# Convolution biases moved out of the loop into PSUM presets, projections split straight from PSUM, and a low-part subtraction moved to GpSimd, in the first stage of an attention and sphere-convolution kernel

## What is computed

```python
x_n = _gn(x)                                            # 4 groups of 2 channels
def _mcl(x, Wm, b):  return einsum('bcgw,cfg->bcfw', x, Wm) + b[None, :, :, None]
def _conv(x, w, b, pad): ...                            # 1x7 over positions, mixes the 8 channels, + b per channel
q = _rope(split_heads(_conv(_mcl(x_n, Wq, bq), q_conv_w, q_conv_b, 3)))
k = _rope(split_heads(_conv(_mcl(x_n, Wk, bk), k_conv_w, k_conv_b, 3)))
v = split_heads(_conv(_mcl(x_n, Wv, bv), v_conv_w, v_conv_b, 3))
```

## Time and profile before

| | |
|---|---|
| Three executions | 1257.97, 1248.56, 1256.05 us; median 1256.05 |
| Profiled execution: time, span | 1258.79 us, 1256.9 us |
| TensorE (matmul) busy in the span | 86% |
| VectorE, ScalarE, GpSimd busy | 74%, 53%, 69% |
| Mean granted TensorE clock | 0.963 of 2.4 GHz |
| `front`: from the start to its last store landed | 0 to about 412.6 us |

### The profile page before, as it was taken

One profiled execution on the slowest core, in us unless ns is written; L12 is line 12 of the kernel. 1 busy time (PEld: TensorE's weight loads), 2 busy tenths in 40 slices (PEclk: granted clock), 3 DMA queues, 4 the chain that ended last, 5 costly groups with the idle time before them and its releaser, 6 DMA issues. The chain is left out here.

```text
span 1256.9 us, 26231 instructions
## 1 busy us (share of the span) xinstructions
PE 1079.0 (86%) x10648; PEld 590.9 (47%) x10648; DVE 933.5 (74%) x1225; ACT 663.2 (53%) x1110; POOL 871.2 (69%) x812
## 2 busy tenths in 40 slices
PE   0299999999894699899998999999988589899998
PEld 0177777777673123333333333333333345355553
DVE  3789999999764798788888888888872584544344
ACT  1555555555442066666666666666666223346345
POOL 0467776777583489899998899988999007937900
PEclk9899999999998589999999999999999799899999
DMA  9725244332644555527171736254000599875661
GB/s 305 238 83 161 76 124 116 104 94 67 139 105 99 115 77 126 111 55 116 49 121 35 122 65 114 57 94 81 31 19 18 184 354 299 265 228 155 190 214 54
DMA packets 137759, 159.02 MB, mean 127 GB/s; under 512 B 17852, under 2 KB 85708, under 8 KB 137640
## 3 DMA queue, kind: packets, MB, share of 16 engines
q1 hardware_dynamic: 113448, 119.37, 39.6%
q10 hardware_dynamic: 15648, 28.81, 6.6%
q0 software_dynamic: 8544, 9.18, 2.8%
HBM read 106.48 MB, written 52.89 MB: 127 GB/s over the span
## 5 line engine op out<-in xcount | busy, mean ns | idle before, releaser
L1108 POOL TENSOR_TENSOR a_pl<-a_prob 128x512 bf16<-128x512 f32 x416 | 443.1, 1094 | 37.0 <-ACT a_prob L1059 36.4
L1012 DVE TENSOR_REDUCE a_negmax<-a_row 128x1 f32<-128x512 f32 x512 | 334.1, 706 | 60.4 <-PE a_row L939 59.2
L1059 ACT ACTIVATE a_prob<-a_col 128x512 f32<-128x512 f32 x512 | 292.1, 596 | 147.0 <-PE a_col L960 140.7
L710 POOL TENSOR_TENSOR f_yl<-f_y,f_yh 128x768 bf16<-128x768 f32 x80 | 132.8, 1679 | 95.8 <-ACT f_yh L657 95.8
L657 ACT ACTIVATE f_yh<-f_y 128x768 bf16<-128x768 f32 x80 | 67.4, 844 | 139.1 <-DVE f_y L548 121.2
L1023 DVE TENSOR_TENSOR a_pl<-a_prob 128x512 bf16<-128x512 f32 x96 | 123.3, 1285 | 19.2 <-ACT a_prob L1059 19.2
L450 PE MATMUL f_acc<-f_wh,f_xh 128*32 128x384 bf16 x1280 | 110.9, 335 | 29.8 <-DVE f_wl L538 26.5
L939 PE MATMUL a_row<-k,q 96*128 96x512 bf16 x256 | 106.6, 423 | 22.7 <-PEq L202 14.9
L960 PE MATMUL a_col<-a_q,a_k 98*128 98x512 bf16 x256 | 97.9, 388 | 23.2 <-ACT a_prob L1059 19.3
L960 PE MATMUL a_col<-q,k 98*128 98x512 bf16 x256 | 99.8, 390 | 16.1 <-ACT a_prob L1059 14.7
L714 POOL TENSOR_TENSOR f_straight<-f_straight,f_turned 128x832 f32<-128x832 f32 x40 | 107.0, 2675 | 9.4 <-DVE f_turned L565 9.4
(11 more groups left out here) (156 smaller groups left out, 2189.2 us busy)
## 6 DMA issues: line engine op xcount, KB each, us to landing
X<-b_x ACTq DMA_DIRECT2D x16, 526.0 KB, 8.3
q<-in_x SPq DMA_DIRECT2D x8, 1024.0 KB, 7.7
a_v<-V SPq DMA_DIRECT2D x16, 512.0 KB, 4.4
Z<-a_z ACTq DMA_DIRECT2D x32, 256.0 KB, 3.5
b_z<-Z SPq DMA_DIRECT2D x16, 512.0 KB, 11.0
b_x<-in_x SPq DMA_DIRECT2D x32, 256.0 KB, 10.1
b_res<-X SPq DMA_DIRECT2D x38, 208.0 KB
out<-b_y ACTq DMA_DIRECT2D x38, 208.0 KB
```

The source lines that it names most:

```text
L710: nc.gpsimd.tensor_tensor(yl[half][n % 2][:], y[half][:], yh[half][n % 2][:], ALU.subtract).then_inc(yl_done, 1)
L1012: nc.vector.reduce_max(negmax[n % PAIR][:, 0, t:t + 1], row[step % ROWS][:], AX.X, negate=True).then_inc(max_done, 1)
L1059: nc.scalar.activation(prob[sets_done % RING][:, t % QUAD, :], col[step % 2][:], ACT.Exp).then_inc(exp_done, 1)
L1108: nc.gpsimd.tensor_tensor(pl[p][:, r, :], prob[p][:, r, :], ph[p][:, r, :], ALU.subtract).then_inc(lo_pool, 1)
```

## The change

All in `front`:

1. **Presets.** Three pseudo windows (`KINDS` = inner, last, first position) are put in front of the loop. Their y is the projection's bias alone (masked by `edge` for the two end kinds), split into high and low (`bias_high` on ScalarE, `bias_low` on VectorE) and sent through `convolution(0..2)`, with `bias_rows`. ScalarE copies the results to SBUF (`tile_qk`, `tile_v`, the latter adding the V bias). TensorE runs these three convolutions before `projection(0, 0)`.
2. **The loop's convolution** has no bias matmul (24 instead of 28 for Q and K) and accumulates onto a preset accumulator: ScalarE writes the kept results into PSUM before each window (`place_v(n)`, `place_qk(n)`), after `keep_v(n - 1)` and after the rope products of window n - 1.
3. **y.** `evacuate`, the mask and `y` are gone. ScalarE's `y_high` rounds straight from `acc`; `y_low` moves from GpSimd to VectorE and subtracts from `acc`. So `acc[half]` is free only after `y_low`.
4. **q_low** moves from VectorE to GpSimd, ahead of `rope_sum` in each window. `keep_v` is one plain copy.
5. **Preparation.** Statistics have four buffers, so their four loads wait for nothing; chunk 0 is loaded before `band`; the first four weight loads are issued when the third statistics load has landed (before: the second); weight tiles 4 to 7 are split in between the pseudo windows. The zero columns at the ends are cleared by GpSimd (`clear_pad`), and edge chunks are normalised only where they hold data.

The core of the diff:

```diff
+        KINDS = (None, 1, 0)
+        def turn(n):
+            return n + len(KINDS)
@@ TensorE
-                    pe.wait_ge(y_ready, summed(n - 1, half))
+                    pe.wait_ge(yl_done, 2 * turn(n - 1) + half + 1)
...
+                if tiled and i:
+                    pe.wait_ge(tiled_qk, i)
+                if not tiled:
+                    pe.wait_ge(preset_qk, i - len(KINDS) + 1)
...
-                        nc.tensor.matmul(out, ones16[:], bias_rows[:, a]..., start=True, stop=False)
+                        if tiled:
+                            nc.tensor.matmul(out, ones16[:], bias_rows[:, a]..., start=kf == 0, stop=False, ...)
...
+            for i in range(len(KINDS)):
+                convolution(i)
             for n in range(TOTAL):
                 projection(n, 0)
                 projection(n, 1)
@@ VectorE
-            for c in range(QUAD + 1, C, 2):
-                w_low(c)
             v.wait_ge(bias_in, 16 * (C + 3))
...
+            for i in range(len(KINDS)):
+                for half in range(HALVES):
+                    bias_low(i, half)
+                if i % 2 == 0:
+                    w_low(QUAD + 1 + i)
-            for n in range(TOTAL + 2):
+            for n in range(TOTAL + 1):
                 for half in range(HALVES):
                     if n < TOTAL:
-                        evacuate(n, half)
-                if 1 <= n <= TOTAL:
+                        y_low(n, half)
+                if n:
                     rope_products(n - 1)
-                if n >= 2:
-                    q_low(n - 2)
@@ ScalarE
-            act.wait_ge(x_in[1], 16)
+            act.wait_ge(x_in[2], 16)
...
-            for c in range(C):
+            for c in range(QUAD):
                 w_high(c)
             act.wait_ge(bias_in, 16 * (C + 3))
+            act.wait_ge(edge_in, 16)
+            for i in range(len(KINDS)):
+                for half in range(HALVES):
+                    bias_high(i, half)
+                w_high(QUAD + i)
+                tile_qk(i)
+                tile_v(i)
+            w_high(C - 1)
...
+                if 1 <= n <= TOTAL:
+                    keep_v(n - 1)
+                if n < TOTAL:
+                    place_v(n)
+                    place_qk(n)
@@ GpSimd
+            for n in range(TOTAL + 2):
+                if n >= 2:
+                    q_low(n - 2)
+                if 1 <= n <= TOTAL:
+                    rope_sum(n - 1)
```

More of the change, by code:

```diff
@@ L472, in convolution @@
+                            nc.tensor.matmul(out, yh[half][s][:, feat], band_l[:, half, a, :], start=False, stop=False, skip_group_check=loose)
+                            last = nc.tensor.matmul(out, yl[half][s][:, feat], band_h[:, half, a, :], start=False, stop=half == 1, skip_group_check=loose)
                 last.then_inc(qk_full, 1)
-                if m:
-                    pe.wait_ge(v_kept, 2 * m)
+                if tiled and i:
+                    pe.wait_ge(tiled_v, 2 * i)
+                if not tiled:
+                    pe.wait_ge(preset_v, i - len(KINDS) + 1)
@@ L538, in w_low, with y_low, bias_low @@
                 nc.vector.tensor_tensor(wl[c][:], w[c % 4], wh[c][:], ALU.subtract).then_inc(w_lo[1], 1)
[L540 to L552, removed]
+            def y_low(n, half):
+                s = turn(n) % 2
+                v.wait_ge(yh_done, 2 * turn(n) + half + 1)
+                nc.vector.tensor_tensor(yl[half][s][:].rearrange("p (a n) -> p a n", a=2), acc[half][:, :, 0:PART],
+                                        yh[half][s][:].rearrange("p (a n) -> p a n", a=2), ALU.subtract).then_inc(yl_done, 1)
+            def bias_low(i, half):
+                e = KINDS[i]
+                v.wait_ge(yh_done, 2 * i + half + 1)
+                if e is None:
+                    nc.vector.tensor_tensor(yl[half][i % 2][:], bias[half][:], yh[half][i % 2][:], ALU.subtract).then_inc(yl_done, 1)
+                else:
+                    nc.vector.scalar_tensor_tensor(yl[half][i % 2][:], bias[half][:], edge[:, e:e + 1], yh[half][i % 2][:],
+                                                   ALU.mult, ALU.subtract).then_inc(yl_done, 1)
             def rope_products(m):
@@ new lines, in y_high, with bias_high @@
+                act.wait_ge(v_full, turn(n) - 1)
+                nc.scalar.activation(yh[half][turn(n) % 2][:].rearrange("p (a n) -> p a n", a=2), acc[half][:, :, 0:PART], ACT.Copy).then_inc(yh_done, 1)
+            def bias_high(i, half):
+                e = KINDS[i]
+                if i >= 2:
+                    act.wait_ge(v_full, i - 1)
+                if e is None:
+                    nc.scalar.activation(yh[half][i % 2][:], bias[half][:], ACT.Copy).then_inc(yh_done, 1)
+                else:
+                    nc.scalar.activation(yh[half][i % 2][:], bias[half][:], ACT.Identity, scale=edge[:, e:e + 1]).then_inc(yh_done, 1)
@@ new lines, in tile_qk, with tile_v @@
+            def tile_qk(i):
+                e = KINDS[i]
+                act.wait_ge(qk_full, i + 1)
+                if e is None:
+                    nc.scalar.activation(inner_qk[:], acc_qk[:, :, 0:2 * OC].rearrange("p a (m w) -> p a m w", w=OW)[:, :, :, PAD], ACT.Copy).then_inc(tiled_qk, 1)
+                else:
+                    nc.scalar.activation(edge_qk[e][:], acc_qk[:, :, 0:2 * OC], ACT.Copy).then_inc(tiled_qk, 1)
+            def tile_v(i):
+                e = KINDS[i]
+                act.wait_ge(v_full, i + 1)
+                for mh in range(2):
+                    nc.scalar.activation(all_v[2 if e is None else e][:, mh, :], acc_v[0:VR, mh, :], ACT.Identity, bias=v_bias[:, mh:mh + 1]).then_inc(tiled_v, 1)
```

172 lines of the change are left out of this document (101 added, 71 removed).

## The result

Six executions of the changed kernel have a median of 1265.65 us, six of the kernel before 1253.95. The ratio is 1.0071, with a 95% interval of 1.004 to 1.0102: slower by 0.7%, some 9 us. One of the six took 2356.76 us and is left out of the ratio. The profiled execution took 1262.72 us with a span of 1260.9.

A forecast was written before the change was run, and what follows sets the result against it. TensorE and VectorE were both taken as full in the first stage, TensorE pacing the changed loop. Start +25.8, loop -20.7 and behind the loop +0.8 gave +5.9 on 1258.8, 1264.7 us; against the median 1262, range 1246 to 1277.

The forecast's parts named there:

- The start: Preparation before the loop in the first stage: three pseudo convolutions and their queued splitting make it 25.8 us longer.
- S: Start of the first `x_high` in the preparation, 31.67 us before the change, forecast at 31.2.
- T: Time when TensorE starts `convolution(0)` in the preparation, forecast at S + 25.1 us.
- The two estimates for `band`: Load of `band` in the preparation: ready near 25 us if some weights come later, about 29 if they win their share.
- The period: One loop window: TensorE sets the pace, falling from 7.92 to 7.56 us without four bias matmuls.
- The second rival: Loop gets no faster because the preset is late or `y_low` costs 1.91 us: period 8.07, 1281 us, chance 0.15.
- no line of TensorE waiting for a preset: Sign expected in the new trace of the loop: TensorE never waits for ScalarE's preset accumulator.
- The loop: All windows of the first stage: 304.9 us against 325.6, so 20.7 us shorter.
- The V waits: ScalarE's `keep_v` waits for a V store twice in the loop; TensorE loses 5.9 us each, 12 against 14.3 before.
- Behind the loop: After the last window, `q_low(39)` on GpSimd takes 1.7 us against 0.95, costing 0.8 us.
- The first (cheap start, no V waits): Rival: `band` early (-2.7), convolutions at full clock (-4.9), V waits gone (-12): 1242 us, chance 0.12.
- The third (a dearer start): Rival: preparation's convolutions at the lower clock throughout (+6.3) and `band` late (+1.8): 1270 us, chance 0.18.

The follow-up runs named there:

- the first experiment: Changed kernel with only the order of the preparation altered on ScalarE and VectorE: ratio 0.996 to the kernel before, median 1248.57 us, first rope products at 80.80 instead of 97.44.

## Why the prediction was right

The forecast was +5.9 us on the profiled execution and 1262; the medians say 1265.65 and the ratio about +9, inside the range and within 1% of the forecast. The first stage came out 10.9 us longer, though, 5.0 more than forecast. That the profiled execution took 1262.72 us, so near the 1264.7 of the sum, is luck: the two other stages happened to take 6.9 us less.

**The start: +25.8 forecast, +26.6 measured.** S was forecast at 31.2 and was 30.98. T was to be S + 25.1 = 56.3; the first pseudo convolution started at 56.18. `w_low(5)` was to start 9.5 us behind it and started 9.7 behind. The three convolutions took 5.5 to 5.7 us each, forecast 5.5. For the third that was luck in part: the prediction spoke of some 7 us of idling before each, while its own sum leaves 3.5 before the third, and 3.7 was measured; the third then began at a granted clock of 1.00 and had 0.50 only from 80.5 to 83.5 us. The order of the chain was what decided, shown by the first experiment. The two estimates for `band` were 25 and 29; it was used from 27.42. Two slips in the bounds did no harm: an early `band` is worth 31.2 - 28.8 = 2.4 us and not 2.7, and twice 3.9 is 7.8 and not 7.6.

**The period: 7.56 forecast, 7.57 measured.** `y_low` at 0.945 was 0.956; `place_qk` at 0.9 was 0.85; `q_low` on GpSimd, priced between 1.8 and 2.7, was 1.71. `x_low` was priced too high, at 1.93: in the loop of the changed kernel it took 0.71 (524 columns) and 0.97 (536), so VectorE was busy some 4.9 us a window and not 5.9. TensorE was the slower one either way. That VectorE's new instruction with one operand in PSUM would not be slowed beside GpSimd stood on the earlier trace rows. The Trainium skill, SBUF — State Buffer, section "Who interferes with whom", says so too, and the trace agrees: 1.24 ns a column, with GpSimd at work on SBUF. The second rival (the preset or `y_low` sets the pace) is refuted by the experiment that put four matmuls back. The sign "no line of TensorE waiting for a preset" held in the ordinary windows only: TensorE did wait for one behind each V wait and before the last convolution.

**The loop: -20.7 forecast, -15.7 measured.** This is the term that I mis-sized, by 5.0 us. Its parts:

- *The V waits*, forecast at 5.9 us each. ScalarE was late as forecast (7.8 us against 7.5 in the first), and TensorE waited 5.45 us for the preset. That wait is even shorter than the 5.9 forecast. But the long period is 7.5 above the ordinary one, since what followed ran at a lower clock. Windows of the changed kernel around the first wait:

```profile
345.00:350.00 5.00, 1.19 (x32) 0.54 (x20) 0.00 (x0) 0.52 (x1) 0.34 (x1) 1.00 0.59 111
350.00:357.00 7.00, 5.36 (x31) 4.76 (x32) 2.83 (x4) 3.67 (x6) 1.71 (x1) 0.51 0.16 51
```

  After a stretch with 1.2 us of work in 5.0, the granted clock is 0.51 (1.2 GHz) for the next 7 us. They hold the Q and K part of the late convolution, which took 4.35 us from its first matmul (351.64) to the rope products (355.99) against 2.35 at the full clock behind it (361.70 to 364.05); that is the missing 2 us. The Trainium skill, TensorE: Matmul & The Clock Gate, section "HAM oscillation — how this bites in real kernels", describes the clock falling back in waits for a DMA. I had priced this in the start and forgotten it here. At the second one TensorE waited 5.32 us and the period is 7.2 longer. Together 14.7 instead of 12, so 2.7 us.
- *Other windows*: 38 ordinary periods take 2.1 us more than 38 x 7.56. Four windows are longer, by 0.45, 0.23, 0.55 and 0.49: three between windows 8 and 13, where TensorE also makes the statistics of batch 1 and ScalarE its square root, and the one behind the V wait. I had taken one period for all.
- *The last period*: 5.8 instead of 5.6, 0.2 us.

**Behind the loop: +0.8 forecast, 0.0 measured.** From the last rope product to the next stage it is 16.2 us in both kernels. `q_low` on GpSimd costs more there, but `rope_sum` in front of it took 1.94 and not 2.6.

**The rivals.** The first (cheap start, no V waits) did not come true: `band` was used from 27.42, the convolutions did not run at the full clock throughout, and no transfer made the V waits go by itself. Taken away by hand they are worth 14.0 us, where it says 12. The third (a dearer start) did not either: 26.6 us, with convolutions of 5.5 to 5.7 and not 7.6.

## What to carry to other kernels

- Before pricing a preparation step by its own duration, write the streams of the engines side by side and follow one chain: three convolutions of 5.5 us cost 26.6 us, 16.6 of them because steps of the chain stood behind work for a later one. Reordering two loops took back 16.6 us without touching an instruction.
- Where two engines are full, relieving one gives almost nothing (1.9 and 5.9 us), both together 13.7 (without the late periods 2.8, 4.1 and 17.7). Tried one at a time, either edit would have been judged too small to keep.
- A two-deep output buffer behind a queue that also carries a burst of other transfers is a stall that no edit of the compute here removed: look for it by its landing, not by its line.

## What the runs showed of the hardware that I had not expected

- `rope_sum`, unchanged, takes 2.68 us in the kernel before and 2.14 in the changed one; with `q_low` alone moved off VectorE it already takes 2.16. So here a GpSimd instruction on SBUF got faster when VectorE had one instruction less with both operands in SBUF, and `x_low`, of that kind too, fell from 1.93 to 1.51 us in the same run. VectorE's `q_low` took 2.0 us in the loop and 0.96 (768 columns) at 402.09 us, where GpSimd was idle. Which of the two is slowed differs: at 398.37 us `q_low` took only 1.02 beside a `rope_sum` of 2.64, which takes 1.94 alone.
- The low clock after a wait came on top of the wait, about 2 us each time: 5.45 us of waiting, 7.5 us lost, and 5.32 us of waiting, 7.2 lost.
